# A four-layer encoder with routing beside it: streams in two halves, routing placed by a table, masks on GpSimd

## What is computed

```
x: 8 streams x 512 tokens x 128; 16 heads of 8
for i in range(4):                                   # encoder layers
    x = x + mha(layer_norm(x), causal mask + ALiBi)  # q, k, v, softmax, projection
    x = x + ffn(layer_norm(x))                       # 128 -> 512, gelu, -> 128
x = layer_norm(x) * final_w + final_b + x_in
# mixture of experts, 8 experts, top 2, routed by a hyperbolic distance of the normed row
x = x + sum over the two of w_k * (gelu(xn @ W1[e]) @ W2[e])
# then attention with rotary positions (same shape), and a second round of the experts
```

## Time and profile before

| what | value |
|---|---|
| runs | 2682.97, 2682.01, 2673.92 us; median 2682.01 |
| profiled execution | span 2681.7 us from first to last instruction; no other time is given for it |
| TensorE's mean granted clock | 0.938 of full speed |
| busy | PE 86%, DVE 64%, ACT 55%, POOL 34% of the span |
| jobs 3 to 25 | from 242.7 to 1294.5 us |
| jobs 26 to 31 | from 1294.5 to 1651.5 us |

### The profile page before, as it was taken

One profiled execution on the slowest core, in us unless ns is written; L12 is line 12 of the kernel. 1 busy time (PEld: TensorE's weight loads), 2 busy tenths in 40 slices (PEclk: granted clock), 3 DMA queues, 4 the chain that ended last, 5 costly groups with the idle time before them and its releaser, 6 DMA issues.

```text
span 2681.7 us, 106832 instructions
## 1 busy us (share of the span) xinstructions
PE 2307.2 (86%) x46638; PEld 1445.0 (54%) x46638; DVE 1722.7 (64%) x5525; ACT 1464.2 (55%) x2646; POOL 900.5 (34%) x1037
## 2 busy tenths in 40 slices
PE   3689999999999999999998888977878777888973
PEld 1345555555555555555555555766644444546873
DVE  6877777778787787877777763323657667752212
ACT  0357777777777777777655555432244334454431
POOL 6334333334333333434233332323112332232135
PEclk9799999999999999999989989988888889889987
DMA  4253333333433333333212213566422221105764
GB/s 114 80 160 102 110 119 112 115 119 99 136 93 127 107 124 94 120 108 108 71 62 62 76 34 100 164 188 179 127 74 60 65 64 59 59 15 169 223 189 122
DMA packets 162546, 289.02 MB, mean 108 GB/s; under 512 B 28504, under 2 KB 116312, under 8 KB 160344
## 3 DMA queue, kind: packets, MB, share of 16 engines
q1 hardware_dynamic: 153696, 264.23, 32.5%
q0 software_dynamic: 8384, 17.97, 2.4%
HBM read 227.33 MB, written 95.96 MB: 121 GB/s over the span
## 4 chain that ended last, share of the span: by engine, by line
PE 65%; DVE 16%; ACT 8%; issue 5%; POOL 2%; another core or an unknown queue 2%; DMA 2%; SPq 1%; POOLq 0%; ACTq 0%; DVEq 0%
PE bank L481 26%; PE bank L647 10%; PE bank L601 9%; DVE mx L1281 5%; PE bank L787 5%; PE bank L797 5%; ACT big L878 3%; PE bank L665 3%; PE bank L488 2%; ACT OT L884 1%; DVE stats L960 1%; PE bank L609 1%; DVE xn L973 1%; ACT big L946 1%
## 5 line engine op out<-in xcount | busy, mean ns | idle before, releaser
L878 ACT ACTIVATE big<-bank 128x512 f32<-128x512 f32 x1600 | 921.4, 599 | 725.4 <-PE bank L481 665.1
L1281 DVE TENSOR_REDUCE mx<-bank 128x16 f32<-128x512 f32 (+1 forms) x1440 | 902.6, 653 | 461.5 <-PE bank L609 394.5
L481 PE MATMUL bank<-QS,KS 99*32 99x512 bf16 (+3 forms) x10240 | 650.5, 309 | 49.6 <-ACT big L878 39.3
L601 PE MATMUL bank<-KS,QS 96*32 96x352 bf16 (+15 forms) x10240 | 586.3, 292 | 96.8 <-DVE mx L1281 50.5
L1577 POOL TENSOR_SCALAR_AFFINE_SELECT big<-big 128x768 f32<-128x768 f32 (+1 forms) x416 | 254.1, 634 | 649.5 <-ACT big L878 649.5
L601 PEld LDWEIGHTS bank<-KS,QS 96*32 96x32 bf16 x10240 | 242.8, 98 | 393.2 <-issue 174.4
L647 PE MATMUL bank<-big,V 128*9 128x512 f32 (+3 forms) x5120 | 448.0, 447 | 5.5 <-issue 3.2
L481 PEld LDWEIGHTS bank<-QS,KS 99*32 99x32 bf16 x10240 | 218.1, 99 | 213.3 <-ACT big L878 97.2
L609 PE MATMUL bank<-mask_a,ident_b 128*32 128x64 bf16 (+1 forms) x5760 | 305.3, 195 | 5.8 <-issue 5.6
L946 ACT ACTIVATE big<-bank,big 128x256 f32<-128x256 f32 x368 | 150.9, 470 | 270.2 <-PE bank L787 208.9
L787 PE MATMUL bank<-big 128*128 128x256 f32 x736 | 187.5, 400 | 34.0 <-ACT big L931 30.6
(11 more groups left out here) (220 smaller groups left out, 2898.9 us busy)
## 6 DMA issues: line engine op xcount, KB each, us to landing
big<-e_pack SPq DMA_DIRECT2D x92, 578.0 KB
QS<-part_scr SPq DMA_DIRECT2D x480, 96.0 KB
KS<-part_scr SPq DMA_DIRECT2D x480, 96.0 KB
part_scr<-parts SPq DMA_DIRECT2D x80, 384.0 KB
x_rows<-in_alibi SPq DMA_DIRECT2D x47, 384.0 KB, 5.1
y_rows<-in_alibi SPq DMA_DIRECT2D x47, 384.0 KB, 5.8
big<-x_rows SPq DMA_DIRECT2D x92, 128.0 KB
y_rows<-big SPq DMA_DIRECT2D x92, 128.0 KB
```

The costliest lines, as they stand in the source:

```text
L481: last = mm(out[c:c + 32], stationary[:, c:c + 32], moving, start=start, stop=stop)
L601: mm(bk[h * SUB:(h + 1) * SUB, col:col + w], Q[0:ROW_MAX, 4 * quad + h, i * SUB:(i + 1) * SUB], K[0:ROW_MAX, 4 * quad + h, 0:w], start=(co ...
L878: A(dst, src, ACT.Exp).then_inc(exp_done, 1)
L1281: v.tensor_reduce(mx[:, quad, k, 0:w], src, axis=AX.X, op=ALU.max).then_inc(a_used, 1)
```

## The change

1. `CLEARED` becomes 32: POOL clears the exponentials of all encoder jobs; no encoder job has mask matmuls.
2. Jobs are ordered by halves: streams 0 to 3 go through layers 0 to 3 (jobs 0 to 15), then streams 4 to 7 (jobs 16 to 31). A job's layer norm then waits for the FFN sum of the job four before.
3. Routing is placed by `route_at`: stream S below 4 starts at job index 16 + 4 S with the same positions inside the job as before (scatters three positions apart). Streams 4 to 7 have a table of their own, from index 29 to 33, with three DVE steps in each position.
4. PE's waits for a free bank and for DVE's reads follow from these positions (`bank_free`, `ffn_xt`).
5. Rows are cleared with three pairs of copies in a job instead of two. The tail starts five positions ahead of the tiles instead of four.

```diff
-TAIL_LEAD, TAIL_RATE = 4, (2.0, 1.5)
+TAIL_LEAD, TAIL_RATE = 5, (2.0, 1.5)
-        CLEARED = ENC - JOBS + 2
+        HALF = JOBS // 2
+        CLEARED = ENC
+        def stream_of(j):
+            return j // (LAYERS * HALF) * HALF + j % HALF
+        def layer_of(j):
+            return j % (LAYERS * HALF) // HALF
+        def last_job(S):
+            return (S // HALF + 1) * LAYERS * HALF - HALF + S % HALF
+        FIRST_ROUTED = 16
+        LATE = {HALF: dict(load=29 * CHUNKS + 32, bias=29 * CHUNKS + 35, ln1=30 * CHUNKS + 23, root1=30 * CHUNKS + 24,
+                           final=30 * CHUNKS + 25, rows=30 * CHUNKS + 26, ln2=30 * CHUNKS + 32, root2=30 * CHUNKS + 33,
+                           apply=30 * CHUNKS + 36, turn=31 * CHUNKS + 1, ranks=31 * CHUNKS + 16),
...
+                HALF + 3: dict(load=32 * CHUNKS + 20, bias=32 * CHUNKS + 26, ln1=32 * CHUNKS + 31, root1=32 * CHUNKS + 32,
+                               final=32 * CHUNKS + 34, rows=32 * CHUNKS + 35, ln2=32 * CHUNKS + 38, root2=32 * CHUNKS + 39,
+                               apply=33 * CHUNKS + 2, turn=33 * CHUNKS + 4, ranks=33 * CHUNKS + 19)}
+        def route_at(S, what, n=0):
+            if S < HALF:
+                p = (FIRST_ROUTED + 4 * S) * CHUNKS
+                if what == "step":
+                    return p + (23 if n == 0 else 24 + n if n <= 28 else 26 + n)
+                if what == "scatter":
+                    return p + 59 + 3 * n
+                return p + dict(load=-10, bias=-7, ln1=0, root1=1, final=3, rows=4, ln2=7, root2=8, apply=15, turn=17,
+                                columns=18, project=19, squares=20, dots=22, norm=24, picked=52, ranks=54)[what]
+            at = LATE[S]
+            if what in at:
+                return at[what]
+            if what == "step":
+                return at["turn"] + 5 + (n + 2) // 3 if n <= 28 else at["ranks"] + n // 3 - 8
+            if what == "scatter":
+                return at["ranks"] + 3 + (2 * n if S < JOBS - 1 else 4 * n // 3)
...
+            def bank_free(p):
+                i, pos = divmod(p, CHUNKS)
+                pe.wait_ge(v_ready, min(i + 3 if pos > 11 else i + 2, ENC))
+                pe.wait_ge(mT_ready, min(i + 1, ENC))
+                pe.wait_ge(gelu_done, FT * min(i if pos > 29 else i - 1, ENC))
...
                 def lns(b, j):
                     if rope_job:
                         dve.wait_ge(combined, j + 1)
+                    elif layer_of(j) > 0:
+                        dve.wait_ge(f_added, 2 * (b + j - HALF + 1))
                     ln_stats(ln_index(b, j), stream(b, j))
...
-                    for n in range(max(2 * (j - 1), 0), min(2 * j, CLEARS)):
+                    for n in range(max(3 * (j - 1), 0), min(3 * j, CLEARS)):
```

More of the change, by code:

```diff
@@ new lines, in route_at @@
+        def route_at(S, what, n=0):
[14 more added lines that the diff above has]
+                return at["ranks"] + 3 + (2 * n if S < JOBS - 1 else 4 * n // 3)
+            if what == "picked":
+                return at["turn"] + 15
+            return at["turn"] + dict(columns=1, project=2, squares=3, dots=4, norm=5)[what]
@@ L754, in attention @@
                 else:
[L755 to L759, removed]
+                    for step, what in ((route_transposes, "turn"), (route_project, "project"), (route_dots, "dots"),
+                                       (route_ranks, "ranks")):
+                        extras += beside_encoder(step, what)
                 return lambda i, pos: position(base, i, pos, jobs, pass_a, pass_b, extras)
@@ L1375, in attention @@
                 else:
[L1376 to L1379, removed]
+                    for n in range(STEPS):
+                        extras += beside_encoder(lambda S, n=n: route(S, n), "step", n)
+                    for step, what in ((route_layernorm, "ln1"), (final_apply, "final"), (second_layernorm, "ln2"),
+                                       (route_apply, "apply")):
+                        extras += beside_encoder(step, what)
                 return lambda i, pos: position(base, i, pos, jobs, maxima, None, extras)
@@ L1596, in attention @@
                     extras += [(lambda b, j, n=n: first_ln(b, j, n), 2, (17 + 8 * n, 1)) for n in range(2)]
[L1597 to L1606, removed]
+                    for step, what in ((lambda S: route_rsqrt(2 * S), "root1"), (final_bias, "bias"), (final_rows, "rows"),
+                                       (lambda S: route_rsqrt(2 * S + 1), "root2"), (norm_root, "norm"),
+                                       (picked_root, "picked")):
+                        extras += beside_encoder(step, what)
+                    for c in range(2 * TT):
+                        extras += beside_encoder(lambda S, c=c: scatter(S, (c,)), "scatter", c)
                 else:
```

71 lines of the change are left out of this document (30 added, 41 removed).

## The result

The changed kernel takes 2712.57 us (median of 4 runs, 2710.13 to 2716.26) against 2682.49 for the kernel before beside it: ratio 1.0121, interval 1.0100 to 1.0142. It is slower by 1.2%, where I forecast 1.3% faster. Its profiled execution took 2710.13 us with a span of 2708.3, 26.6 more than before.

What follows compares the result with a forecast made beforehand. It took TensorE's queue, waits included, as the bound. Gains of 23.5 (jobs 16 to 29) and 18 (job 30), less 3.6 (job 31) and 2 (transition), gave 36 us: 2647 us, own range 2634 to 2660, whole range 2626 to 2678.

Steps and rivals of the forecast that it cites:

- The mask: Jobs 26 to 31: deleting TensorE's mask matmuls gains 3.7 us a job, 22 in all; GpSimd's selects cost nothing.
- First part: Routing of one stream, layer norms to 16 DVE steps: costs 7.3 us per stream, bounds 5 and 9.
- Second part: Rest of a stream's routing steps, ranks, eight scatters: 6.9 us before, 3 once spread, bounds 1 and 7.
- overlap and burst: Jobs 27 to 29: two streams' DVE work at once, five scatters in a row; spreading removes both, 6.9 to 3.
- the clock in each first part: Job 26: clock drop after the wait ahead of the dots, 3.4 us, kept inside the 7.3 per stream.
- Jobs 30 and 31: Job 30 falls from 60.5 to 42.5, gain 18; job 31 rises from 49.1 to 52.7, loss 3.6.
- the signs of being wrong: P times V waiting for selects, longer plain jobs, slower small DVE steps, or job 30 and 31 savings returning beside tiles.
- Copies: Three pairs of row-clearing copies in 16 jobs: cost 0, covered by idle DMA before the load of the maxima.
- rival B: About the same, 2679: second part 6.9 and first 9, or copies delay maxima 2 us in 16 jobs; chance 0.14.
- The streams' new order: Layer norm needs the FFN sum of four jobs before: cost 0, bound under 6 us over 28 jobs.
- A: Slower, 2706: clears queue on POOL behind operations awaiting DVE, so P times V waits, 6 us per routed job; chance 0.08.
- C: Half the gain, 2661: GpSimd selects hold DVE's small routing steps at the shared port, 14 us; chance 0.18.

Runs made afterwards that it cites:

- e1: The changed kernel with TensorE doing the causal mask again from job 16 on; 2735.65 us, ratio to before 1.0206.
- e2: The kernel before with GpSimd clearing the exponentials of all encoder jobs and a tail lead of 5; 2672.11 us, ratio to before 0.9957.
- e3: The changed kernel without the encoder's 64 scatters, each replaced by a one-column write on GpSimd; 2681.87 us (one run).
- e9: The e7 kernel without the encoder's 64 scatters, each replaced by a one-column write on GpSimd; 2647.92 us (one run).
- e5: The changed kernel with streams 0 to 3 routed in consecutive jobs from 16 on, so two streams' parts overlap; 2687.54 us, ratio to before 1.0042.
- e4: The kernel before with three pairs of row-clearing copies per job instead of two; 2687.26 us, ratio to before 1.0016.
- e7: The changed kernel with routing of streams 0 to 3 over five jobs, small steps in VectorE's idle stretch at position 28; 2670.11 us, ratio 0.9966.

## Why the prediction was wrong

**The mask, 22 us: the term was mis-sized, and it led the next ones astray.** I priced the mask by the distance between starts in PE's queue, 3.7 us a job, and bounded it by 3.8 and 10.9. A plain job pays 2.2 (e1), below both bounds. In a routed job the exchange of the mask for the selects brings 0.5 to 0.8 (e2: 0.8 in job 26, 1.6 over jobs 27 to 29, 0.8 in job 30), figures that a single execution hardly carries. PE waits there anyway for DVE or ACT, which may be the reason; no run shows it. All of it together is worth some 5 us in the profiled executions (start of the rope jobs 1944.8 instead of 1950.4) and 12 in the medians. I had subtracted 3.7 from every routed job to get the price of routing, which made routing look 3 us cheaper per job than it is.

**First part, 7.3 us, bounds 5 to 9: too small.** It is 10.2 without the mask (e2) and 8.8 to 11.5 in the changed kernel. Mostly the subtraction above.

**Second part, "3 instead of 6.9": this is the step that failed.** It is 9 to 12 us in a job of its own, with 1.6 to 3.0 behind it, above my upper bound of 7. I had argued that its two largest terms were tied to overlap and burst. The packed kernel refutes the first: overlapped, both parts cost 16.7, spread 23.6. The scatters in threes refute the second: a scatter costs the same in a row of three or alone. My bounds came from a remainder of two overlapped parts, and a remainder says nothing of what the part costs by itself: whatever the two share counts once there and twice when they are taken apart.

**What is counted twice is above all the clock.** My sum had 3.4 us for the clock in each first part, 13.6 in all, and nothing for it in a second part or in the job behind one. By the rows it is 46.7 us, so up to 33 of the 53 by which jobs 16 to 29 came out wrong. A second part with the job behind it costs 14.6, 11.0 and 13.9 us (streams 0 to 2), and 8.6, 5.2 and 8.9 of that is length times (1 - clock).

**What the second part consists of besides.** In the changed kernel scatters take some 5.7 us per stream (e3: 22.9 / 4), their share of the clock included. That the rest is steps of DVE held by POOL and late results behind them is likely and not shown: e3 leaves 4.5 to 7 us, and the small steps were held about as long in the kernel before. With everything moved out of DVE's busy stretch a stream without scatters costs 8.6 (e9), of which 3.0 are PE's own transposes, projection and dots.

**Jobs 30 and 31.** Job 30 saved 13.9 of my 18: its 42.5 was 1.3 to 1.5 too low for a job with nothing left over (43.8 and 44.0 in e5 and e3, at the full clock), and with the end of stream 3's part it took 46.6 at a clock of 0.93, which accounts for the difference. Job 31 and the tiles lost 12.3, of which I had 5.6; 7.9 in job 31, where the denser routing of stream 4 lies, 4.4 after it. No run takes that apart. In jobs 30 and 31 and the tiles together, 407 us against 408, the saving in job 30 came back, as I had named it among the signs of being wrong.

**Copies.** "Cost 0" was wrong by about 4 us; my 2 us in each of 16 jobs (rival B) would have been 32. The wait that I watched, the load of the maxima, isn't the one that came.

**The streams' new order** cost nothing that shows: jobs 2 to 15 differ by little more than e4's copies.

**The rivals.** A's mechanism was there in the form of POOL's order (a root behind a scatter, and a wait of 2.3 us for `xn`), and P times V waited for a clear once, 2.1 us in job 30 (PE's waits there name `big` L1613 of POOL; it is 1.3 in e5, at 43.8 us) and 0.9 in job 31; in the routed jobs 16 to 29 no such wait is among PE's. C had the right mechanism: clears do hold VectorE. I spread 14 us over eight streams, with 0.3 to 0.6 a step; per stream two steps that I could find meet a clear, `chosen` for 0.70 (where another operation of POOL held it before) and one of the layer norm for 1.0 us more than alone. Yet the run without clears (e1) gained nothing in the routed jobs, so C isn't the loss. B's premise, that the cost lies in routing and not in overlap, was right and still too mild: none of the rivals had spreading as the loss. That is what was missing. One reading of mine was loose: the cast of `parts` in the earlier trace rows ends at 1360.72, 0.29 after POOL's operation (1360.43), not with it.

## What to carry to other kernels

A price got by subtracting from a stretch where several things overlap is a marginal price: it holds while they stay together. Before you move a part to a place of its own, look for the same part alone in the trace, or bound it from above by the whole excess of its job. Putting late work in different jobs paid here for each delay again, and far more for the clock that fell in each of them (eleven jobs instead of five): read the granted clock of single jobs before and after, and give it a term of its own in the sum. What helped is to put the work where its engine is idle (e7), not where there is less of it.

## What the runs showed of the hardware

**PE stands still during scatters, with nothing to wait for.** In job 21 of the changed kernel, POOL and then PE:

```profile
1157.04 1.03 POOL L1570 DMA_INDIRECT x_rows<-xnR,slots  x1 [0.20 <-issue]
1158.38 0.97 POOL L1570 DMA_INDIRECT x_rows<-xnR,slots  x1 [0.31 <-issue]
```

```profile
1158.16 0.19 PE L644 MATMUL bank<-mask_a,ident_b 128*32 128x32 bf16 x4
1160.00 0.40 PE L515 MATMUL bank<-QS,KS 99*32 99x512 bf16 x4 [1.65 <-issue]
```

ACT's next exponential starts 1.60 us after the last one ended in the same stretch, though its matmul had ended at 1158.1. In job 21 of e3, without scatters, PE has no such gap. The Trainium skill (SBUF — State Buffer, "Who interferes with whom") says that PE and ACT never wait on anyone for SBUF; these gaps are not explained by its port rule, since two engines that have no part in it stop together. Whether the signals between engines, the fetch of instructions or the descriptors are slow then, no run here shows. Whether the gap of 0.83 us behind the clearing copies (738.6 to 739.5 us) is of the same kind isn't shown either: the 16 DMA engines were 94% busy from 731 to 737 us, but 26% from there to the gap and 19% in it.

**A step of 128 x 32 elements took six times as long** (1153 against 192 ns) beside an operation of POOL, in all four streams of the changed kernel, and 1.15 us in the kernel before.

**A clear on GpSimd held single steps of VectorE to its end.** `chosen` (128 x 64) took 922 against 219 ns, and one step of the layer norm (128 x 128) up to 1485 against a median of 341 ns; in e1, where GpSimd clears nothing in these jobs, no step of that line takes over 522 ns.

**The granted clock fell in jobs in which PE's longest wait was 2.1 us** (0.91 in job 16, 0.97 in job 20), and fell again in each of the four periods.
